# A two-layer transformer kernel with 58 unused matrix products per pair of sequences added in three places of TensorE's queue

## What is computed

```python
x = x + attn0(layernorm(x))   # 16 heads of 16, softmax taken in blocks of 256 keys, no bias
x = x + ffn0(layernorm(x))    # 1024 hidden units, ternary weights, relu(h)**2
x = x + attn1(layernorm(x))   # 16 heads of 16, softmax over 512 keys, biases
x = x + ffn1(layernorm(x))    # 8 trees of 255 nodes: silu(logit) on the path taken, else 0
```

## Time and profile before

| | us |
|---|---|
| median of 3 runs | 3438.83 |
| lowest, highest | 3438.67, 3439.48 |
| the profiled execution | 3437.46 |
| its span, first to last instruction | 3435.4 |

### The profile page before, as it was taken

The page is one execution under the profiler, slowest core; times in us unless marked ns, Lnnn a source line. Parts: engine busy times, 40 slices in busy tenths (PEclk is TensorE's granted clock), DMA queues, the critical chain, the costliest instruction groups (busy, mean ns, idle before and its releaser), DMA issues.

```text
span 3435.4 us, 48439 instructions
## 1 busy us (share of the span) xinstructions
PE 3023.4 (88%) x18980; PEld 1336.3 (39%) x18980; DVE 2224.0 (65%) x4099; ACT 1923.9 (56%) x2559; POOL 909.4 (26%) x1206
## 2 busy tenths in 40 slices
PE   0488899988999899988998889998899989998899
PEld 0124255242643326333362424524254232633336
DVE  0784866757566676766667486675856667576664
ACT  0274654737557474655746566474754737456474
POOL 0013223141321414113141232314132141321313
PEclk9589999999999899998999999999999989999899
DMA  3000000000100001000010000100001000100000
GB/s 116 21 21 19 21 26 32 21 19 21 40 27 12 25 16 50 27 2 29 24 38 27 20 21 22 36 21 19 21 29 39 12 19 21 46 28 5 29 18 19
DMA packets 92691, 90.88 MB, mean 26 GB/s; under 512 B 15757, under 2 KB 89877, under 8 KB 92453
## 3 DMA queue, kind: packets, MB, share of 16 engines
q1 hardware_dynamic: 92465, 87.79, 7.5%
HBM read 17.48 MB, written 8.39 MB: 8 GB/s over the span
## 4 chain that ended last, share of the span: by engine, by line
PE 64%; DVE 23%; ACT 5%; issue 2%; POOL 2%; SPq 2%; DMA 0%; DVEq 0%
PE ps L986 12%; PE ps L1053 12%; PE ps L1031 12%; PE ps L1231 8%; DVE nmax L748 8%; DVE nmax L751 7%; PE ps L1011 6%; PE ps L992 4%; PE ps L1202 3%; PE ps L1042 3%; ACT probs L524 2%; SPq L263 2%; PE ps L999 2%; PE ps L1222 1%; PE ps L1059 1%
## 5 line engine op out<-in xcount | busy, mean ns | idle before, releaser
L524 ACT ACTIVATE probs<-ps 128x1024 f32<-128x1024 f32 x1024 | 1043.1, 1025 | 398.1 <-PE ps L1042 390.1
L1031 PE MATMUL ps<-kst,qst 48*128 48x512 f16 x2048 | 751.8, 416 | 183.0 <-DVE nmax L748 77.9
L751 DVE TENSOR_REDUCE nmax<-ps 128x1 f32<-128x512 f32 x1024 | 651.0, 684 | 239.8 <-PE ps L1031 238.8
L748 DVE TENSOR_REDUCE nmax<-ps 128x2 f32<-128x512 f32 x1024 | 650.8, 684 | 219.4 <-PE ps L1031 215.5
L1042 PE MATMUL ps<-qst,kst 54*128 54x512 f16 x2048 | 725.9, 411 | 5.0 <-ACT probs L524 5.0
L1053 PE MATMUL ps<-probs,vn 128*32 128x512 f32 x4096 | 544.0, 604 | 6.6 <-ACT oT L512 6.6
L1031 PEld LDWEIGHTS ps<-kst,qst 48*128 48x128 f16 x2048 | 156.4, 94 | 870.8 <-DVE nmax L748 362.4
L420 POOL TENSOR_TENSOR probs<-probs 127x512 f16<-127x512 f32 (+1 forms) x256 | 292.2, 1162 | 519.7 <-ACT probs L650 519.7
L650 ACT ACTIVATE probs<-probs 127x512 f16<-127x512 f32 (+1 forms) x256 | 161.2, 630 | 350.5 <-DVE probs L940 346.9
L1231 PE MATMUL ps<-wout,probs 127*128 127x256 f16 (+1 forms) x3072 | 357.2, 273 | 0.0
L986 PE MATMUL ps<-hT,win 128*127 128x512 f16 (+1 forms) x1536 | 354.3, 380 | 2.6 <-ACT probs L626 2.6
(11 more groups left out here) (115 smaller groups left out, 3200.1 us busy)
## 6 DMA issues: line engine op xcount, KB each, us to landing
qst<-parts SPq DMA_DIRECT2D x384, 64.0 KB, 2.6
kst<-parts SPq DMA_DIRECT2D x384, 64.0 KB, 2.6
x<-in_x SPq DMA_DIRECT2D x16, 512.0 KB, 4.0
probs<-x SPq DMA_DIRECT2D x16, 512.0 KB, 3.0
out<-probs SPq DMA_DIRECT2D x16, 512.0 KB, 3.0
qst<-nrow SPq DMA_DIRECT2D x256, 12.0 KB
qst<-in_winT SPq DMA_DIRECT2D x1, 2040.0 KB
oT<-in_wfcT SPq DMA_DIRECT2D x1, 1024.0 KB
```

The lines of the kernel that those rows point to most:

```text
L524: nc.scalar.activation(probs[:, g % 2, 2 * hf:2 * hf + 2, s % G, :], ps[:, 2 + 2 * hf:4 + 2 * hf, :], ACT.Exp).then_inc(exp_rd, 1)
L748: nc.vector.tensor_reduce(nmax[:, u, 2 * tt + half, :, slot], bank[tt % 2].rearrange("p (a s) -> p a s", s=BLK), AX.X, ALU.max, negate=Tru ...
L751: nc.vector.tensor_reduce(nmax[:, u, 2 * tt + half, 0, slot:slot + 1], bank[tt % 2], AX.X, ALU.max, negate=True).then_inc(max_rd, 1)
L1031: mm(bank[tt % 2], qst[lo:hi, ai % 2, e // 2, tt * P:(tt + 1) * P], kst[lo:hi, ai % 2, e // 2, :], start=True, stop=True).then_inc(max_ps, 1)
```

## The change

A helper keep_going(k, free) issues k products in a row: the identity idb as the loaded operand, 512 columns of wfc as the moving one, written into a bank that is given. They have no semaphore, neither waited for nor raised, and nothing reads what they write before it is overwritten.

```diff
--- before.py
+++ after.py
@@ -1069,6 +1069,11 @@
                     ins = by_token(bank[P_BANK[ph][half]][:, i * D:(i + 1) * D], wo[ph // 4], 2 * half + i, hT[ph % 2])
                 ins.then_inc(proj_ps, 1)
 
+
+            def keep_going(k, free):
+                for _ in range(k):
+                    mm(free, idb[:], wfc[:, HI, 0, 0:S], start=True, stop=True)
+
             def pair_of_tiles(b, ph, n, ahead, s, hf):
                 for kt in (2 * hf, 2 * hf + 1):
                     if ahead:
@@ -1094,7 +1099,11 @@
                     pair_of_tiles(b, ph, n, ahead, s, 0)
                     if s >= G:
                         weighted(n, ai, s // G - 1, s % G)
+                    elif s < 2:
+                        keep_going(3, bank[6])
                     pair_of_tiles(b, ph, n, ahead, s, 1)
+                    if s == 0:
+                        keep_going(2, bank[6])
                     if s == 1:
                         maxima_rows(n, 1)
                         transposed(b, nxt, 0)
@@ -1282,17 +1291,21 @@
                 for c in range(5, M0):
                     hidden(b, c)
                     project(b, c - 2)
+                keep_going(2, bank[2])
                 project(b, 6)
                 project(b, 7)
                 pe.wait_ge(attn_sb, n1 * T + T)
                 attn_T(n1, 1, 0)
                 attn_T(n1, 1, 1)
+                keep_going(5, bank[2])
                 pe.wait_ge(aT_hi, n1 * KD + KD)
                 pe.wait_ge(aT_lo, n1 * KD + KD)
                 projected(n1, 1, 0)
                 projected(n1, 1, 1)
+                keep_going(7, bank[2])
                 transposed(b, 4, 0)
                 transposed(b, 4, 1)
+                keep_going(6, bank[2])
                 hT_read(b, 4, 0)
                 hT_read(b, 4, 1)
                 qk_unit(n2, 4, 0)
@@ -1342,11 +1355,15 @@
                 lead_tiles(n2, 2, 10)
                 project(b, 14)
                 lead_tiles(n2, 2, 11)
+                keep_going(3, bank[2])
                 project(b, 15)
                 pe.wait_ge(qk_sb, n2 * 4 + 4)
                 maxima_rows(n2, 0)
+                keep_going(3, bank[2])
                 lead_tiles(n2, 2, 12)
+                keep_going(4, bank[2])
                 lead_tiles(n2, 2, 13)
+                keep_going(4, bank[2])
                 attention_even(b, 4)
                 attention_odd(b, 5)
 
@@ -1424,8 +1441,11 @@
                     maxima_rows(n4, 0)
                 tree_sum(b, TREES - 1)
                 if more:
+                    keep_going(2, bank[6])
                     lead_tiles(n4, 0, 12)
+                    keep_going(4, bank[6])
                     lead_tiles(n4, 0, 13)
+                    keep_going(2, bank[6])
                 pe.wait_ge(x_upd, (b + 1) * (2 * PHASES))
```

## The result

| | before | after |
|---|---|---|
| median, us | 3438.99 (4 runs) | 3407.06 (4 runs) |
| lowest, highest | 3438.67, 3439.48 | 3403.13, 3410.76 |
| ratio, 95% interval | | 0.9907 (0.9890 to 0.9924) |
| profiled execution, its span | 3437.46, 3435.4 | 3410.74, 3408.7 |
| mean granted clock | 0.938 | 0.972 |

The change makes the kernel 0.93% faster, 32 us; 3415 us was forecast, within 3380 to 3434. The four runs of after lie at 3403.1, 3403.4, 3410.7 and 3410.8, far more apart than those of before. The profiled one is of the upper pair, so what its trace shows adds up to the 26.7 us between the two spans; no trace shows what the two runs at 3403 did otherwise.

What follows compares the result with a forecast made beforehand. Half-clock stretches were taken to cost where TensorE is on the chain of waits. Terms -16.8, -9, +6.4, -8.4, +3, +1 sum to -23.8 us: profiled 3437.46 to 3413.7, plus 1.37 for the median, 3415 us; range 3380 to 3434.

Steps and rivals of the forecast that it cites:

- First place: L1285 ff. of before: 20 products in gaps keep the clock up, transposes start earlier; -2.1 us per pair.
- Second fall: Clock fall at 742.6, no product put there; expected to go in 6 pairs of 8, -9 us in all.
- Second place: Start of phase 4, 22 products: six on VectorE's chain cost +1.3 us, 0.5 comes back; net +0.8 per pair.
- rival 2: Only the first place works and exposed products (+1.3 per pair) eat most of it; 3439 us, no change; chance 0.14.
- late return of the clock: Clock back later than the trace's 0.3 us behind L1011 x6; +0.2 us at 15 places, +3.
- Third place: Start of phase 0, 16 products, 7 of 8 pairs: maxima_rows, transposes and VectorE's awaited product come earlier; -1.2 us per pair.
- Small terms: Late returns of the clock, +3 us; eight products at half clock in phase 0 of pair 0, +1 us.
- Rival 1: The clock holds right through both attention starts; 3382 us; chance 0.15.
- Rival 3: Products with an identity loaded do not hold the clock and are pure cost; +4.7 per pair, 3475 us; chance 0.09.

Runs made afterwards that it cites:

- third_only: Kernel before plus only the 2 + 4 + 2 products behind the trees and the 8 in steps 0 and 1 of phase 0; 3417.14 us, ratio 0.9935.
- exposed_only: Kernel before plus only 3 products ahead of project(15) and 3 behind maxima_rows; 3452.27 us, ratio 1.0039.
- covered_no_exposed: Changed kernel without the 3 products ahead of project(15) and 3 behind maxima_rows, plus 4 each in steps 2 and 3 of every even phase; 3374.18 us.
- closed: covered_no_exposed plus 5 products between hidden(10) and project(8), minus the 2 ahead of lead tile 12; 3370.66 us, ratio 0.9801.
- covered: Changed kernel plus 4 products each in steps 2 and 3 of every even phase, the six exposed products kept; 3385.86 us, ratio 0.9846.
- loaded_wfc: Changed kernel with 128 columns of wfc as the loaded operand instead of the identity idb; 3412.46 us, ratio 0.9919.
- rows48: Changed kernel with all 456 added products using 48 of the 128 rows; 3438.09 us, ratio 0.9995.

## Why the prediction held, and where not

**First place.** Forecast -2.1, measured -1.78 per pair. The mechanism is the one named: clock up, products under the waits, normalisation of phase 3 next. Up to the start of the transposes behind it the gain is 2.06 us in pair 1 (725.06 less 711.73, against 729.12 less 713.73). But these transposes then stand 1.09 us on the chain, as they do behind the wait at 721.12, instead of the 0.87 they had while TensorE came to them without a pause. That is most of what is missing.

**Second fall.** I gave it 6 pairs of 8, it went in all 8: 12.6 us instead of 9. In third_only and exposed_only it comes and goes between pairs with the same instructions around it, so nothing near it decides; that it is the position in time is what is left. How often it goes was luck: in covered_no_exposed it was 5 of 8.

**Second place.** Forecast +0.8: exposed +1.3, back 0.5. Measured +1.39 for the six (27.73 against 26.34) and only 0.05 back from step 0 to step 5, together +1.34, which is rival 2's figure. The mean hides two terms. Here each start of phase 4 of the profiled run is cut at the start of its first L1011 x6 and held against the same pair of before:

| pair | 0 | 1 | 2 | 3 | 4 | 5 | 6 | 7 |
|---|---|---|---|---|---|---|---|---|
| clock falls, us behind step 0 | 10.0 | 13.8 | 8.9 | 9.3 | 6.0 | 9.2 | 6.0 | 9.2 |
| step 0 to L1011 x6, us against before | -0.9 | -1.5 | -0.9 | -0.9 | 0.0 | -0.9 | 0.0 | -0.9 |
| clock back, us behind the start of L1011 x6 | 2.6 | 3.5 | 4.9 | 5.3 | 4.5 | 5.2 | 4.5 | 5.1 |
| L1011 x6 to step 5, us against before | 0.0 | +0.2 | +0.9 | +1.1 | +0.7 | +1.0 | +0.7 | +1.0 |

Up to L1011 x6 0.75 us comes back in the mean, more than the 0.5 forecast. It is nothing only in pairs 4 and 6, where the clock falls ahead of maxima_rows; in the chain of pair 4 stand

```profile
1988.18 0.60 PE ps L1037 x4
1988.78 1.05 PE ps L999 x4
...
1996.00 2.72 PE ps L1011 x6
```

just the lengths of the earlier trace rows. Behind that start 0.69 us is lost again: the clock is back after 4.5 to 5.3 us in pairs 2 to 7, where it took 2.9 to 3.1 in those pairs before, and the work in between stays at half clock. So the term that was off is the late return of the clock, +0.2 per place in the forecast and +0.69 in phase 4.

**Third place.** Forecast -1.2, measured -1.65. Up to L1011 x6 it is -1.32. In that are the 2 products ahead of lead tile 12, exposed with +0.44, which I had hidden beside tree_residual; closed, which leaves them out, has them back (27.01 to 26.58). The other -0.33 lie behind L1011 x6: in pairs 2 to 7 the clock is back 2.0 to 2.9 us after its start instead of 3.6. In this chain of after, maxima_rows and transposes have 0.32 and 0.59 us, and VectorE's own work follows:

```profile
987.42 0.43 PE ps L1075 x2
987.86 0.54 PE ps L1031 x2
988.39 0.97 PE ps L1075 x4
...
995.59 0.32 PE ps L1037 x4
995.91 0.59 PE ps L999 x4
```

The prediction had 0.45 for the transposes at full clock and so 0.14 too much to gain: its 0.45 at 713.73 is not a whole group of four at full clock but the part after which the chain goes on with ScalarE.

**Small terms.** The late returns, forecast +3 over 15 places, came to +5.5 in phase 4 and -2.3 in phase 0, together +3.2. That the sum agrees is luck: two errors of opposite sign. I allowed +1 for pair 0, whose phase 0 took 58.37 us against 58.40; the 1.3 us at the program's start are something else.

**Sum.** -16.8, -9, +6.4, -8.4, +3, +1 against -14.2, -12.6, +5.1 (11.1 less 6.0), -9.3, +3.2, and +1.3 at the program's start: -23.8 against -26.5 in the spans. Errors of up to 4 us a term, in both directions. The rest up to the 32 us between the medians is the spread of after's runs.

**Rivals.** Rival 1 (the clock holds through, 3382) was not the case; covered, covered_no_exposed and closed, which cover steps 2 and 3 as well, come to 3386, 3374 and 3371. Rival 2 fell with the second fall and the third place, but its second place came true. Rival 3 fell in loaded_wfc and at 722. rows48 shows what products cost that do not hold the clock: 1.5 us at the start of phase 0 in most pairs, where rival 3 had 2.6.

What stays open: why single attention starts still fall in closed, and the spread of the runs of after. Both would fit the program standing in one of two positions against the instants at which the clock changes, as the alternating pairs of 401.7 and 403.9 us in covered do, but no run set a position by itself.

## What to carry to other kernels

Read the granted clock in windows before pricing a wait: a wait of 1.7 to 2 us on TensorE may cost as much behind it as in itself. Fill it with full-array products into a bank that is free, as many as the gap holds at full clock, and none where TensorE's next step already has its input, since there they cost their own time here and kept nothing up. Cover the whole low stretch up to the next dense work, or the work that you meant to speed up may still run at half clock; and price what happens until the clock is back as a term of its own, for each place.

## What the runs showed of the hardware

- The same number of columns with 48 instead of 128 rows does not keep the clock up where most other products have 48 or 54 rows: 3438 against 3407 us.
- Whether the loaded operand was an identity or weights made no difference: 3407 and 3412 us, with intervals that overlap, and the same 144 us of half clock.
- The same gap at project(8) brought the clock down in 8, 1, 4, 3 and 0 pairs of 8 (before, third_only, exposed_only, covered_no_exposed, after), within one kernel in some pairs and not in others.
- The clock came back 2.9 to 3.1 us after the start of the first L1011 x6 of phase 4 in pairs 1 to 7 of before, and 4.5 to 5.3 us after it in pairs 2 to 7 of after.
